# Ternary FFN on one core: a third product of each pair by seven inner products, two rings of weight blocks, one mixing bank, and loads issued at other places

## What is computed

```python
def _L0_cond_ref(x, embedding, W0, b0, W1, b1, W2, b2, weight, bias_k):
    h = jax.nn.gelu(embedding @ W0 + b0, approximate=False)
    h = jax.nn.gelu(h @ W1 + b1, approximate=False)
    att = jax.nn.softmax((h @ W2 + b2) / T, axis=-1)
    agg_w = jnp.einsum('bk,koi->boi', att, weight[..., 0])
    agg_b = att @ bias_k
    return jnp.einsum('boi,bih->boh', agg_w, x) + agg_b[:, :, None]

def _bitlinear(x, w):
    scale = jnp.mean(jnp.abs(w))
    q = jnp.round(jnp.clip(w / (scale + EPS), -1.0, 1.0))
    return x @ (q * scale).T

def _L0_ffn_ref(hidden_states, w_gate, w_up, w_down):
    gate = _bitlinear(hidden_states, w_gate)
    up = _bitlinear(hidden_states, w_up)
    return _bitlinear(gate * up, w_down)

# x: (64, 64, 1024) f32; w_gate, w_up: (2752, 1024); w_down: (1024, 2752)
x = x + _L0_ffn_ref(_L0_cond_ref(x, cond_128, ...), w_gate, w_up, w_down)
```

## Time and profile before

| | |
|---|---|
| median of 3 runs | 1718.07 us (1717.92 to 1718.26) |
| the profiled execution's own time | 1718.81 us |
| its span | 1716.8 us, mean granted clock 0.997 |
| PE busy | 1692.5 us (99%), 13792 matmuls |
| weight loads (PEld) busy | 1218.2 us (71%) |
| VectorE (DVE) busy | 1178.6 us (69%) |
| ScalarE (ACT) busy | 656.3 us (38%) |
| GpSimd (POOL) busy | 90.5 us (5%) |
| DMA | 228.31 MB, mean 133 GB/s |

### The profile page before, as it was taken

The page is one execution under the profiler, slowest core; times in us unless marked ns, Lnnn a source line. Parts: engine busy times, 40 slices in busy tenths (PEclk is TensorE's granted clock), DMA queues, the critical chain, the costliest instruction groups (busy, mean ns, idle before and its releaser), DMA issues.

```text
span 1716.8 us, 35301 instructions
## 1 busy us (share of the span) xinstructions
PE 1692.5 (99%) x13792; PEld 1218.2 (71%) x13792; DVE 1178.6 (69%) x1960; ACT 656.3 (38%) x1253; POOL 90.5 (5%) x148
## 2 busy tenths in 40 slices
PE   7999999999999999999999999999999999999999
PEld 5554555977768686795958969487785968679694
DVE  6888896575766757676684766857576675766464
ACT  6877741321424234241433414343252423424140
POOL 0010004441100000000000000000000000000000
PEclk9999999999999999999999999999999999999999
DMA  8667625521343122620326202352134412353121
GB/s 344 250 225 253 239 94 201 208 79 50 145 162 139 56 86 110 245 84 28 121 103 224 100 32 98 121 220 84 52 143 150 152 56 75 120 186 103 37 94 49
DMA packets 84562, 228.31 MB, mean 133 GB/s; under 512 B 11152, under 2 KB 26064, under 8 KB 84272
## 3 DMA queue, kind: packets, MB, share of 16 engines
q1 hardware_dynamic: 80144, 207.91, 33.4%
q0 software_dynamic: 3664, 18.03, 2.8%
q10 hardware_dynamic: 592, 0.09, 0.0%
HBM read 191.31 MB, written 34.68 MB: 132 GB/s over the span
## 4 chain that ended last, share of the span: by engine, by line
PE 90%; DMA 5%; SPq 2%; DVE 1%; issue 1%; ACT 1%; DVEq 0%; ACTq 0%
PE ps L976 36%; PE ps L1094 25%; PE ps L747 18%; PE ps L988 9%; DMA g_r<-wsub 4%; PE ps L1053 2%; PE ps L853 1%; DMA xa<-in_x_dram 1%; SPq L583 0%; SPq L545 0%; SPq L590 0%; ACT msk L1236 0%; DVE xr L2010 0%; SPq L535 0%; DVE msk L1666 0%
## 5 line engine op out<-in xcount | busy, mean ns | idle before, releaser
L976 PE MATMUL ps<-yp,wgT 128*128 128x256 f16 x3204 | 716.3, 273 | 0.8 <-issue 0.5
L976 PE MATMUL ps<-wuT,wgT 128*128 128x256 f16 x3204 | 716.2, 273 | 0.0
L1094 PE MATMUL ps<-wdT,inter 128*128 128x512 fp8e4 x1960 | 434.2, 379 | 0.0
L1094 PEld LDWEIGHTS ps<-wdT,inter 128*128 128x128 f16 x1960 | 191.3, 98 | 226.8
L976 PEld LDWEIGHTS ps<-yp,wgT 128*128 128x128 fp8e4 x3204 | 313.9, 98 | 37.9 <-issue 2.6
L976 PEld LDWEIGHTS ps<-wuT,wgT 128*128 128x128 fp8e4 x3204 | 313.8, 98 | 35.9
L2010 DVE SCALAR_TENSOR_TENSOR xr<-ps,osc,xr 128x512 f32<-128x512 f32 x210 | 157.0, 749 | 126.3 <-PE ps L1094 102.2
L1420 ACT COPY raw<-ps 128x512 f32<-128x512 f32 (+1 forms) x77 | 43.7, 568 | 306.6 <-PE ps L976 306.4
L1927 DVE TENSOR_TENSOR wdT<-ps,msk 128x512 f32<-128x512 f32 (+1 forms) x77 | 51.4, 668 | 78.6 <-PE ps L976 78.6
L1992 DVE TENSOR_TENSOR inter<-inter 128x1024 f16<-128x1024 f32 x70 | 85.3, 1219 | 0.0
L988 PE MATMUL ps<-yp,wgT 128*128 128x128 f16 x456 | 75.6, 219 | 7.2 <-DMA g_r<-wsub 7.2
(11 more groups left out here) (273 smaller groups left out, 2303.6 us busy)
## 6 DMA issues: line engine op xcount, KB each, us to landing
wgT<-wcomb SPq DMA_DIRECT2D x70, 896.0 KB, 4.7
wdT<-dcomb SPq DMA_DIRECT2D x14, 2240.0 KB, 8.8
xa<-in_x_dram SPq DMA_DIRECT2D x8, 2048.0 KB, 12.8
xr<-in_x_dram SPq DMA_DIRECT2D x32, 512.0 KB, 13.1
out_dram<-xr SPq DMA_DIRECT2D x64, 256.0 KB, 2.0
wcomb<-xa POOLq DMA_DIRECT2D x17, 448.0 KB, 3.0
g_r<-wsub SPq DMA_DIRECT2D x54, 128.0 KB, 3.9
xr<-in_L_ffn_w_down_dram SPq DMA_DIRECT2D x9, 512.0 KB, 6.2
```

The costliest lines, as they stand in the source:

```text
L976: last = nc.tensor.matmul(out, w, operand(i, OPERAND[what])[:, k, :], start=(start and h + k + i == 0), stop=(k == KQ - 1 and i == 1), ski ...
L1094: last = nc.tensor.matmul(bank[:, :], x, wd_block(p, BLOCK[what]), start=(what in ("P1", "P2", "P5") and q + i == 0), stop=(q == GRP - 1 a ...
```

## The change

P1 too is done by seven inner products, in pairs 1 to 5 and 7 to 9 (`AHEAD`), in chunks 2 to 7. Its parts stand ahead, in the body of the pair before: `ahead_a` before `inner_d`, `ahead_b` after it, `ahead_g` between the halves of P7, and `ahead_d` in its own pair after `inner_a`. They have their own space (`lower1` in ps7, `upper1` in what was the third slot of the ring), copies on ScalarE (`ahead1` to `ahead3`) and an addition on VectorE (`inner_upper1`).

The ring has two slots in place of three, and each slot is two rings: the blocks of P1, P6, P5, P2 and P7 (`EARLY_B` = 5, 640 KB) are loaded when P7 of the pair two before is done, those of P4 and P3 (256 KB) when its P3 is. Mixing in chunks 2 to 6 for the next chunk has one bank, ps6. The down weights of group 0 are loaded after pair 3's late blocks, the residual after pair 4's and 5's. VectorE's tail makes three sets of activation sums in place of two, and `lo_a` stands in a chunk's pairs at the end of a body.

```diff
-    RING = 3
+    RING = 2
+    EARLY_B = 5
...
-    INNER, TH = ('P2', 'P5'), P
+    INNER, TH = ("P1", "P2", "P5"), P
     NI = len(INNER)
+    AHEAD = (1, 2, 3, 4, 5, 7, 8, 9)
...
+        def mixed(c, k):
+            return YB[k % 2 if isinstance(c, int) and c <= FIRST else 0]
...
             def next_pairs(c):
...
-                for p, before in ((0, NPR - 1), (1, NPR), (2, NPR - 2)):
-                    sp.wait_ge(s_m3, NS * (c - FIRST) + before + 1)
-                    ring_load(p)
+                sp.wait_ge(s_m7, n + NPR)
+                early_load(1)
+                sp.wait_ge(s_m3, n + NPR)
+                late_load(1)
+                sp.wait_ge(s_m7, n + NS)
+                early_load(0)
+                sp.wait_ge(s_m3, n + NS)
+                late_load(0)
...
             def pairs(c):
                 for p in range(RING, NS):
-                    if p > RING and inners(c, p - 1):
-                        sp.wait_ge(s_done[INNER[-1]], NS * (c - FIRST) + p - 2)
-                        sub_load(c, p - 1)
-                    sp.wait_ge(s_m3, NS * (c - FIRST) + p - RING + 1)
+                    sp.wait_ge(s_m7, n + p - 1)
+                    if inners(c, p):
+                        sub_load(p)
                     if isinstance(c, int) and c == FIRST:
-                        sp.wait_ge(s_subd, NI * (p - RING + 1))
-                    ring_load(p)
+                        sp.wait_ge(s_subd, NI * (p - 1))
+                    early_load(p)
+                    sp.wait_ge(s_m3, n + p - 1)
+                    late_load(p)
+                    if p == 3 and not (isinstance(c, int) and c == FIRST):
+                        sp.wait_ge(s_dn, DN * FIRST + ND2 * (c - FIRST))
+                        down_load(0)
+                    if p in (4, 5):
+                        load_res(c, p - 4)
...
             def chunk(c):
                 next_x(c)
-                load_res(c)
-                if inners(c, 2):
-                    sub_third(c)
                 pairs(c)
                 next_pairs(c)
                 store2(c)
-                sp.wait_ge(s_dn, DN * FIRST + ND2 * (c - FIRST) + ND2)
-                down_load(0)
...
+                if k and not (isinstance(c, int) and c <= FIRST):
+                    pe.wait_ge(s_yv, KH * c + k)
+                elif k >= 2:
                     pe.wait_ge(s_yv, KH * c + k - 1)
...
+            def ahead_d(c, p):
+                pe.wait_ge(s_jr, ahead_count(c, p))
+                waited(c)
+                bank = inner_bank(p, "P1")
+                inner("P1", p, bank[:, 0:TH], IA12, (0, 1))
+                inner("P1", p, bank[:, 2 * TH:3 * TH], IS4, (1, 1))
+                inner("P1", p, bank[:, TH:2 * TH], IA22, 3).then_inc(s_m1, 1)
...
-                    product(c, p, "P1")
+                    if not ahead(c, p):
+                        product(c, p, "P1")
                     if inners(c, p):
                         inner_a(c, p)
+                        if ahead(c, p):
+                            ahead_d(c, p)
...
-                        inner_d(c, p)
-                        product(c, p, "P7")
+                        if ahead(c, p + 1):
+                            ahead_a(c, p + 1)
+                            inner_d(c, p)
+                            ahead_b(c, p + 1)
+                            product(c, p, "P7", 0)
+                            ahead_g(c, p + 1)
+                            product(c, p, "P7", 1)
+                        else:
+                            inner_d(c, p)
+                            product(c, p, "P7")
...
-                steps = (("sum", S1),), (("lo", A11),), (("lo", A21),), (("sum", S3),), (("sum", S2),), (("inner", 0),), \
-                        (("lo", A12),), (("sum", S4),), (("lo", A22),), (("lower", 0),), (("lo", S1),), \
-                        (("inner", 1), ("lo", S2)), (("lo", S3),), (("lower", 1),), (("lo", S4),), ()
+                steps = (("sum", S1),), (("lo", A11),), (("inner", 0),), (("lo", A21),), (("sum", S3),), (("lower", 0),), \
+                        (("sum", S2),), (("inner", 1),), (("lo", A12),), (("sum", S4),), (("lower", 1),), (("inner", 2),), \
+                        (("lo", A22),), (("lo", S1),), (("lower", 2), ("lo", S2)), (("lo", S3), ("lo", S4))
...
+                        if p:
+                            lo_a(c, p - 1)
+                    if ahead(c, p + 1):
+                        inner_upper1(c, p + 1)
```

More of the change, by code:

```diff
@@ L395, in inners, with ahead, sub_loads, sub_count @@
                 return ()
-            return INNER[0:1 if p == 0 else NI]
+            return INNER[1:2 if p == 0 else 3]
+        def ahead(c, p):
+            return not (isinstance(c, int) and c == FIRST) and p in AHEAD
+        def sub_loads(p):
+            return ("P1",) * (p in AHEAD) + INNER[1:2 if p == 0 else 3]
+        def sub_count(p):
+            each = [len(sub_loads(n)) for n in range(p % 2, NPR, 2)]
+            return sum(each), sum(each[:p // 2 + 1])
         def inner_x(what, i, s):
@@ L512, in adaln_ternary_ffn @@
         s_ring = [sem(f"s_ring{i}") for i in range(RING)]
+        s_ringL = [sem(f"s_ringL{i}") for i in range(RING)]
         s_subt, s_subd = sem("s_subt"), sem("s_subd")
@@ L578, in _, with load_res @@
             load_bias(1)
-            def load_res(c):
-                for t in range(NT):
+            def load_res(c, i):
+                for t in (2 * i, 2 * i + 1):
                     sp.wait_ge(s_st[t], 16 * HB * c)
@@ L676, in _ @@
                 chunk(c)
-            load_res(NC - 1)
-            sub_third(NC - 1)
             pairs(NC - 1)
@@ L1384, in hi_quarters @@
                 for s in range(8):
-                    if s == S4:
-                        hi_inner(c, 0)
+                    if s in (A12, S4):
+                        hi_inner(c, int(s == S4))
                     hi_quarter(c, s)
-                for q in range(1, NI):
-                    hi_inner(c, q)
+                hi_inner(c, 2)
             first = 2 * NPR + 1
@@ L1468, in inner3, with ahead_count, ahead1, ahead2 @@
                     last = nc.scalar.copy(inner_bank(p, what)[:, TH:2 * TH], lowers[:, q, 0])
-                last.then_inc(s_e3, 1)
+                last.then_inc(s_inner_copy, 1)
+            def ahead_count(c, p):
+                return len(AHEAD) * (c - FIRST - 1) + AHEAD.index(p) + 1
+            def ahead1(c, p):
+                act.wait_ge(s_ahead, 3 * ahead_count(c, p) - 2)
+                nc.scalar.copy(inner_bank(p, "P1")[:, 0:TH], lower1[:, 0]).then_inc(s_ahead_copy, 1)
+            def ahead2(c, p):
+                act.wait_ge(s_ahead, 3 * ahead_count(c, p) - 1)
+                nc.scalar.copy(upper1[:, 0], lower1[:, 0]).then_inc(s_ahead_copy, 1)
+            def ahead3(c, p):
+                act.wait_ge(s_ahead, 3 * ahead_count(c, p))
+                nc.scalar.copy(upper1[:, 1], lower1[:, 0])
+                nc.scalar.copy(inner_bank(p, "P1")[:, TH:2 * TH], lower1[:, 0]).then_inc(s_ahead_copy, 1)
             def hi_inner(c, q):
@@ L1498, in pairs @@
                         magnitudes(c + 1, 2 * (p - 2) + 1)
+                    if ahead(c, p + 1):
+                        ahead1(c, p + 1)
                     if p:
                         hi_blocks(c, p - 1)
+                    if ahead(c, p + 1):
+                        ahead2(c, p + 1)
+                        ahead3(c, p + 1)
                     copy_p167(c, p)
```

166 lines of the change are left out of this document (106 added, 60 removed).

## The result

| | before | changed |
|---|---|---|
| median | 1718.16 us (1717.92 to 1721.2, 4 runs) | 1703.07 us (1701.61 to 1704.49, 4 runs) |
| profiled execution, span | 1718.81, 1716.8 us | 1703.82, 1702.0 us |

The ratio is 0.9908 (95% interval 0.9891 to 0.9925): faster by 15.1 us. 1701.0 was forecast, inside 1699.5 to 1710.

What follows compares the result with a forecast made beforehand. TensorE, busy 1692.5 of 1716.8 us, was taken as the bound, so only less work or fewer idle stretches help. 8.7 us from P1 plus 8.5 from loads made 17.2, giving 1701.0 us, range 1699.5 to 1710.

Steps and rivals of the forecast that it cites:

- P1 by inner products: In 8 pairs of each of 6 chunks, 28 short matmuls replace 16 long ones: 0.182 us less, 48 times, 8.7 us.
- the 24: Run of 24 inner 128x128 matmuls in the old trace, 55.8 ns each, taken as pitch for new runs of 36 and 28.
- Handshakes: ScalarE copies and VectorE addition for P1's inner products stay hidden from TensorE, 0.5 to 0.9 us left each step; cost 0.
- Mixing bank, ring and tail: One mixing bank (some 0.8 us left), two ring slots and a third set of sums in the down group's tail: cost 0.
- Loads: With 2.4 MB in place of 6.7 ahead of pair 2's sub blocks, the stall in chunks 2 to 6 goes: 8.5 us.
- the true loss: The weight loads' 8.5 us at the five stalls, taken as their real price rather than TensorE's own 7.2 us.
- the margin of 1.4: In steady state, early blocks land 5.3 to 6.3 us after a body's start, needed at 7.7: at least 1.4 us left.
- at worst 2 us once: In chunk 1, pair 2's early blocks land near 311 to 313, needed at 315: cost 0, at worst 2 us once.
- GpSimd's 30 sets: In chunk 1 GpSimd makes 30 sets, not 20, at 3.7 us: 11 us a pair against bodies of 12.2.
- Lost handshakes: Rival: handshakes or late outputs cost 0.1 to 0.2 us in each laced pair, 5 to 9 us; 1706 to 1710, chance 0.12.
- A moved stall: Rival: pair 2's or 4's early blocks land 1 to 2 us late in five or six chunks; 1707 to 1710, chance 0.09.
- Two slots are too few: Rival: early blocks take over 7.7 us, TensorE stands at `ahead_a` 18 times; landing at 9 us gives 1724; chance 0.05.

Runs made afterwards that it cites:

- loads only: The kernel before with only the residual's and group 0's down-weight loads moved behind pairs 4 to 6; 1710.18 us, ratio 0.9926.
- P1 whole: The changed kernel with P1 as 16 matmuls of 128x256 in all pairs, the rest kept; 1710.45 us, ratio 0.9929.
- the second run: The changed kernel run again with nothing altered, on another set of runs beside the kernel before; 1702.62 us, ratio 0.9887.
- the fourth kernel: The changed kernel with chunk 1's load of group 0's down weights also moved behind pair 3; 1702.44 us, ratio 0.9884.
- e3_loads_back: The changed kernel with the residual and group 0's down loads put back at a chunk's start and end; 1765.76 us.
- e7_tail: The changed kernel with each low part of activation sums in down group 1's tail cut into 8 VectorE pieces; 1702.82 us.

## Why the prediction was right

**P1 by inner products.** Forecast 8.7 us, measured 8.4 (0.176 in place of 0.182 a pair), net of the wait in chunk 7. The pitch taken from the 24 held in runs of 28 and 36.

**Handshakes.** Cost 0, as said, but with half the slack: at `ahead2`, named there as the next late item, 0.28 us instead of 0.53. The count had taken the copy as needed when the half of P7 before it *ends*, at 618.42 in the chain; the next matmul starts at 618.26, 0.16 us sooner, and the rest, about 0.1 us, is not accounted for here. The mixing bank's slack was counted in the same way: 0.6 for 0.8.

**Mixing bank, ring and tail.** Cost 0: the tails of `loads only` and `P1 whole` differ by 0.05 us. The tail bore another 0.47 us a set.

**Loads.** Forecast 8.5, measured 9.4, but not term by term: the five stalls are worth 7.7, and 1.7 is a fall of the clock behind the longest of them, which the forecast did not have. That the weight loads' 8.5 was "the true loss" did not hold; it lies between their figure and TensorE's 7.2. The two errors have opposite signs, so some of the agreement of the sum (17.35 for 17.2) is luck. Early blocks took 5.1 us for the 3.9 estimated, which uses 1.2 of the margin of 1.4. Pair 4's had been counted against the 9.5 us of a body with mixing; chunk 7 has no mixing, there they are asked for after 7.7, and they were late by 0.3 us. What the forecast had allowed as "at worst 2 us once" in chunk 1 came, as 0.6.

**The term left out.** VectorE's slowing by GpSimd in chunk 1, 0.8 us in the profile of the changed kernel, 1.0 in the second run and 1.4 in the fourth kernel. The forecast counted GpSimd's 30 sets against the time in which they had to be ready, not what they do to VectorE beside them. This, pair 2's 0.6 and the clock at the program's start (1.1, scatter) make up the 2.55 us by which the changed kernel is behind at the mark; the forecast was 2.1 too low.

**The rivals.** Lost handshakes: no such wait in chunks 2 to 7. A moved stall: not in the five or six chunks that the rival had, but in chunk 7, 0.3 us in the profile and up to 0.9 in other runs. "Two slots are too few" needed early blocks later than 7.7 us after a body's start; with the old order of loads (`e3_loads_back`) it is what happens in pair 2, and it gives 1765.76. So the change's two halves aren't independent: P1's inner products need the moved loads.

## What to carry to other kernels

A wait's price is more than TensorE's row of it: five waits of 7.2 us cost 7.7, and one clock that fell behind the longest of them another 1.7. A margin that holds in a loop's bodies is to be counted again for a last chunk that leaves part of the work out. A slack counted in ends of matmuls is too large by what a matmul takes over its pitch (here 0.16 us); cutting one copy into 4, 8 and 16 pieces measured the limit twice, at 0.54 and 0.55 us of copy, with no other change. When a side engine gets more work, ask not only whether it is done in time but what runs beside it: a single wait that holds GpSimd back during a critical chain of VectorE brought chunk 1's down group 1.5 us sooner.

## What the runs showed of the hardware

- The granted clock after an idle stretch of TensorE: 1.00 after waits of 0.92 to 1.67 us, 0.72 over the 6 us that begin in the middle of one of 1.97 us, 0.50 after 8.7 us. At 0.50 a 128x128 matmul's pitch was 109 ns (3.93 us for 36).
- VectorE beside a busy GpSimd: f32 to f16 of 128x1024 from 1.22 to 1.65 us, bf16 addition of 128x512 from 0.42 to 0.86. GpSimd's fp8 operation of 128x256, begun 0.07 us after one of VectorE's, from 0.65 to 1.65.
- Further pieces of a cut operation cost 64 ns each, on ScalarE (1.21 - 0.45 = 0.76 us for 12) and on VectorE (1.65 - 0.69 = 0.96 for 15); for the 7 further pieces of `e7_tail` it is 0.47 us, 67 ns each.
